# Column spreads as transposes of a broadcast column, logit columns inside the values' product, and a new static order in a four-layer graph network

## The chip, the cores and the metric

One core of one Trainium2 chip. The program is written engine by engine, with its semaphores and the order of all steps fixed by hand-kept tables. The metric is the device time of one execution in microseconds; lower is better.

## The reference

The input is 16 graphs of 512 nodes with 128 features, `x`, and an integer adjacency matrix `adj` (512 x 512 per graph). Four layers follow one another, each on a layer-normed, rectified copy of the residual stream:

```python
h = jnp.maximum(_layernorm(x, axis=-1), 0.0)
x = x + _L0_gnn_ref(h, adj, L0_gnn_W, L0_gnn_a)
h = jnp.maximum(_layernorm(x, axis=-1), 0.0)
x = x + _L1_gnn_ref(h, adj, L1_gnn_W, L1_gnn_b, L1_gnn_a)
h = jnp.maximum(_layernorm(x, axis=-1), 0.0)
x = x + _L2_gnn_ref(h, adj, L2_gnn_a0, L2_gnn_a1, L2_gnn_a2, L2_gnn_a3, L2_gnn_bias)
h = jnp.maximum(_layernorm(x, axis=-1), 0.0)
x = x + _L3_gnn_ref(h, adj, L3_gnn_weight, L3_gnn_w_ih, L3_gnn_w_hh, L3_gnn_b_ih, L3_gnn_b_hh)
```

The first layer is graph attention with one head, the second the same with four heads of 32 columns:

```python
Wh = jnp.einsum('bnf,of->bno', h, W)
s1 = Wh @ a1
s2 = Wh @ a2
e = jax.nn.leaky_relu(s1[:, :, None] + s2[:, None, :], negative_slope=ALPHA)
att = jax.nn.softmax(jnp.where(mask, -jnp.inf, e), axis=-1)
out = jnp.einsum('bij,bjo->bio', att, Wh)
```

`s1` is a number for each row of the logits (the source), `s2` one for each column (the target). The third layer takes a sigmoid of weighted inner products of the rows, chosen by the kind of edge, and the fourth runs three steps of a gated recurrent cell on the sums over neighbours.

## The kernel before, in words

A graph's 512 nodes lie as C = 4 chunks of 128 on the partitions. The work of a graph is cut into some 170 named steps in four stages: A (first layer), L (logits and softmax of the second layer), B (the rest of the second layer and the third), C (recurrent cell). All stages of different graphs overlap: while graph g is in C, graph g+1 is in L and B and graph g+2 in A. Each engine (TensorE, VectorE, ScalarE, GpSimd) runs the steps strictly in the order that `in_order` gives it: it sorts all steps of all graphs by `BEGIN[stage][graph] + WHEN[engine][step]`. These numbers are keys that set the order, not times. An engine whose next step isn't ready waits, with all that is queued behind it. SyncE loads `x` and the transposed adjacency, GpSimd the two other copies of the adjacency; ScalarE's queue issues the output's store (step `store`).

The steps that the text speaks of, with their lines:

- `rowsN` (N = 0 to 3) turns the normed rows: four transposes on TensorE (`turn_rows`, L936) after all four norm chunks (`normN_0` to `_3` on ScalarE, L394, after GpSimd's power and product, L363 and L365), then a copy to `hT` on ScalarE (L399).
- The logits need the target number spread over all 128 partitions: a row of 512 targets, the same in each partition. `dst0` (L961) and `dst1` to `dst4` (L1005) get it as a full product of the turned rows with `dst_rep`, the target's weight column repeated 128 times, into one PSUM bank; ScalarE copies it to `spread` (L411, L450).
- `src0` (L941 by `project`, four products of one column) gives the first layer's source numbers, which VectorE scales into `s1_lift` (L682); `values0` (L941, four products of 128 columns) gives the values, which ScalarE copies (L416). `values1` (L1009, L1013) gives the second layer's values and its four source columns, 132 columns a chunk, behind one tiny product for a count of edges; VectorE adds the bias (L739), scales the sources (L741) and reads the count (L746).
- `m`/`n` (VectorE, masked maximum, L642), `top`, `below`, `max` (tiny, L650 to L659), `u`/`v` (VectorE logits L663, then ScalarE's exponential L423, L460), `t`/`q` (TensorE, four transposes, L948, then ScalarE's copy to `pT`, L428, L468), `sum0`, `sum1` (L981, L1040).
- `x2` turns the second layer's result on TensorE (L1049), `scaled` and `x2` finish it on VectorE (L796, L802); `mean3` is the last VectorE step of the fourth layer norm (L638); `split` (ScalarE L508, VectorE L865) cuts the normed rows in two parts for `agg` (L1117, L1120), the sums over neighbours. `hidden_*` and `joint_*` (L1102, L1105) are the cell's products, `turn` (L1142) its state turned.
- `s`, `w` are the third layer's slope, hyperbolic tangent and products (L836, L492, L843, L1088); `z` (L1061) its inner products.

PSUM has eight banks. `a_bank` serves all of stage A one after the other, `l_bank0` and `l_bank1` all of stage L.

## Time and profile before

| | |
|---|---|
| three runs | 1064.18, 1065.93 (median), 1067.51 us |
| the profiled execution's own time | 1066.04 us |
| its span in the profile | 1063.9 us |
| granted TensorE clock, mean | 0.967 of 2.4 GHz |
| TensorE busy | 954.6 us (90%) |
| VectorE busy | 892.3 us (84%) |
| ScalarE busy | 864.0 us (81%) |
| GpSimd busy | 132.6 us (12%) |

Busy times are unions of an engine's instructions. Durations in a row hold an instruction's whole latency; instructions in a stream follow each other more closely than they last, so the rate of a stream is read from the chain of waits or the starts in the timeline. A TensorE product of fp32 shows as two matmul records, a transpose and an fp32r product as one.

### The profile page before, as it was taken

What the parts mean: (1) busy time and instruction counts of PE and PEld (TensorE: products, weight loads), DVE (VectorE), ACT (ScalarE), POOL (GpSimd) and SP (SyncE); (2) the same over time, 40 slices, a digit from 0 to 9 for tenths busy, and PEclk for the clock granted to TensorE, in tenths of its full rate; (3) what the DMA queues carried; (4) which work ended last, traced back from release to release, by engine and by line L of the source; (5) the groups of instructions that cost most, each with busy time, mean ns of one, the idle gap of its engine ahead of it and who ended that gap; (6) DMA issues with size and microseconds to landing.
All of it is one profiled execution on the core that took longest, in us unless ns stands there. A gap on an engine that the chain in (4) does not pass through costs nothing.

```text
span 1063.9 us, 16086 instructions
## 1 busy us (share of the span) xinstructions
PE 954.6 (90%) x5024; PEld 609.6 (57%) x5024; DVE 892.3 (84%) x2710; ACT 864.0 (81%) x1860; POOL 132.6 (12%) x170
## 2 busy tenths in 40 slices
PE   4588998999989899999989899998989999998866
PEld 3455565666566566656556566656656665655443
DVE  5296989899898979899897989989897989979543
ACT  3367888979888897988888897988889798887742
POOL 1102011010202011020201201020201101010000
PEclk8558999999999999999999999999999999999989
DMA  2401204021210403121220402121030302111000
GB/s 72 109 1 39 72 11 109 11 61 52 68 51 14 106 11 77 44 60 51 56 64 10 110 11 60 60 61 51 15 105 11 79 31 61 50 40 51 1 11 10
DMA packets 42477, 52.32 MB, mean 49 GB/s; under 512 B 1296, under 2 KB 25872, under 8 KB 42384
## 3 DMA queue, kind: packets, MB, share of 16 engines
q0 software_dynamic: 16896, 25.17, 10.7%
q1 hardware_dynamic: 17040, 21.83, 6.5%
q10 hardware_dynamic: 8448, 4.20, 1.3%
q8 instruction: 44, 0.72, 0.3%
q14 instruction: 49, 0.40, 0.1%
HBM read 55.39 MB, written 4.19 MB: 56 GB/s over the span
## 4 chain that ended last, share of the span: by engine, by line
PE 52%; DVE 28%; ACT 10%; issue 6%; POOL 3%; DMA 0%; DVEq 0%; SPq 0%; ACTq 0%; POOLq 0%
PE l_bank L948 7%; DVE probs L642 6%; PE a_bank L981 6%; PE x_bank L1040 4%; PE a_bank L948 3%; PE h_bank L1102 3%; ACT hn L394 3%; PE r_bank L1102 3%; PE r_bank L1105 3%; DVE sess L843 3%; DVE sess L836 3%; PE h_bank L1105 3%; PE n_bank L1105 3%; DVE probs L663 3%; POOL rstd L363 2%
## 5 line engine op out<-in xcount | busy, mean ns | idle before, releaser
L663 DVE SCALAR_TENSOR_TENSOR probs<-spread,s_lift,probs 128x512 f32<-128x512 f32 x320 | 237.4, 747 | 4.0 <-DVE rmax L642 0.5
L642 DVE CUSTOM_DVE_ANT_0 probs<-spread,mask 128x512 f32<-128x512 f32 x320 | 211.8, 684 | 2.4 <-ACT spread L450 2.3
L363 POOL TENSOR_TENSOR rstd<-var_eps,power 128x4 f32<-128x4 f32 x64 | 88.0, 1375 | 882.5 <-DVE var_eps L636 603.0
L460 ACT ACTIVATE probs<-probs,shift_p 128x512 f32<-128x512 f32 x256 | 185.7, 725 | 5.7 <-DVE shift_p L659 5.7
L468 ACT ACTIVATE pT<-l_bank 128x512 f32<-128x512 f32 x256 | 151.8, 600 | 46.5 <-PE l_bank L948 46.3
L948 PEld LDWEIGHTS l_bank<-ident,probs 128*128 128x128 f32 x1024 | 124.3, 144 | 73.8 <-issue 46.0
L948 PE MATMUL l_bank<-ident,probs 128*128 128x128 f32 x1024 | 150.5, 278 | 6.1 <-ACT probs L460 5.1
L394 ACT ACTIVATE hn<-x,shift,rstd 128x128 f32<-128x128 f32 x192 | 80.5, 492 | 26.1 <-POOL shift L365 26.0
L1005 PE MATMUL l_bank<-hT,dst_rep 128*128 128x512 f32 x128 | 73.6, 658 | 12.1 <-ACT pT L468 8.5
L870 DVE SCALAR_TENSOR_TENSOR hid_n<-r_t,hid_n 128x512 f32<-128x512 f32 x48 | 33.1, 689 | 57.8 <-ACT r_t L518 57.8
L981 PE MATMUL a_bank<-values,pT 128*128 128x128 f32 x512 | 65.7, 286 | 0.7 <-ACT pT L428 0.7
L1088 PE MATMUL y_bank<-hn,sess 128*128 128x128 f32 x512 | 61.6, 278 | 4.2 <-DVE sess L843 4.1
L1088 PEld LDWEIGHTS y_bank<-hn,sess 128*128 128x128 f32 x512 | 58.4, 192 | 11.9 <-DVE sess L843 11.9
L981 PEld LDWEIGHTS a_bank<-values,pT 128*128 128x128 f32 x512 | 63.0, 202 | 2.0 <-ACT pT L428 2.0
L1040 PE MATMUL x_bank<-pT,values 128*32 128x512 f32 x512 | 58.2, 595 | 0.7 <-ACT pT L468 0.7
L450 ACT ACTIVATE spread<-l_bank 128x512 f32<-128x512 f32 x64 | 38.4, 600 | 23.4 <-PE l_bank L1005 23.4
L948 PEld LDWEIGHTS a_bank<-ident,probs 128*128 128x128 f32 x256 | 29.9, 149 | 44.5 <-ACT pT L428 35.8
L948 PE MATMUL a_bank<-ident,probs 128*128 128x128 f32 x256 | 44.4, 300 | 9.7 <-ACT probs L423 5.6
L460 ACT ACTIVATION_READ_ACCUMULATOR probs<-probs,shift_p 128x1 f32 x256 | 51.8, 202 | 0.0
L1105 PE MATMUL r_bank<-aggT,gi_w 128*128 128x512 f32 x96 | 49.4, 596 | 0.0
L1105 PE MATMUL h_bank<-aggT,gi_w 128*128 128x512 f32 x96 | 49.1, 593 | 0.0
L1105 PE MATMUL n_bank<-aggT,gi_w 128*128 128x512 f32 x96 | 49.1, 593 | 0.0
(175 smaller groups left out, 1956.5 us busy)
## 6 DMA issues: line engine op xcount, KB each, us to landing
adjt_i<-in_adj_t SPq DMA_DIRECT2D x16, 1024.0 KB, 5.2
edges<-in_adj POOLq DMA_DIRECT2D x16, 1024.0 KB, 5.9
adj_h<-in_adj POOLq DMA_DIRECT2D x16, 512.0 KB, 7.7
xin<-in_x SPq DMA_DIRECT2D x16, 256.0 KB, 2.9
out<-out_sb ACTq DMA_DIRECT2D x16, 256.0 KB, 3.8
weights_sb<-in_weights SPq DMA_DIRECT2D x1, 840.0 KB, 4.7
```

The lines of the kernel that those rows point to most:

```text
L363: g.tensor_tensor(rstd[n][:], var_eps[n][:], power[:], op=ALU.pow).then_inc(pool_step[n], 1)
L394: s.activation(hn[n][:, c, :], rows[:, c, :], ACT.Relu, bias=shift[n][:, c:c + 1], scale=rstd[n][:, c:c + 1]).then_inc(hn_ready[n], 1)
L460: s.activation(row, row, ACT.Exp, bias=shift_p[:, head, c:c + 1], accum_out=den[:, head, c:c + 1]).then_inc(probs_ready, 1)
L468: s.activation(pT[:, head - 1, :, c * P:(c + 1) * P], l_banks[unit % 2][:, :].rearrange("p (j i) -> p j i", j=C), ACT.Copy).then_inc(pT_co ...
L642: return v.tensor_tensor_reduce(out=row, in0=spread_row, in1=mask, scale=1.0 / LIFT, scalar=-3e38, op0=ALU.subtract, op1=ALU.max, accum_ou ...
L663: v.scalar_tensor_tensor(row, spread_row, source, row, ALU.min, ALU.subtract, reverse1=True).then_inc(ready, 1)
L948: last = t.transpose(dst[:, j * P:(j + 1) * P], row[:, j * P:(j + 1) * P], ident[:])
L981: last = t.matmul(a_bank[:, c * P:(c + 1) * P], pT0[:, j, c * P:(c + 1) * P], values0[:, j, :], start=(j == 0), stop=(j == C - 1))
L1005: t.matmul(l_banks[head % 2][:, :], dst_rep[:, head, :], hT[1][:, :], start=True, stop=True).then_inc(dst_ready, 1)
L1040: last = t.matmul(x_bank[h * HD:(h + 1) * HD, :], values1[:, j, h * HD:(h + 1) * HD], pT[:, h, j, :], start=(j == 0), stop=(j == C - 1), s ...
L1088: last = t.matmul(y_bank[:, c * P:(c + 1) * P], sess[:, j, c * P:(c + 1) * P], hn[2][:, j, :], start=False, stop=(j == C - 1), skip_group_ ...
L1105: t.matmul(bank[:, :], gi_w[:, layer, gate * D:(gate + 1) * D], aggT[:, :], start=start, stop=True).then_inc(gi_ready, 1)
```

## The change

- Both layers' spreads are no products any more. The target numbers now come as a column of the values' product (so they lie on the partitions), and a spread is four transposes of that column read 128 times (`spread_column`).
- `values0_w` holds the value weights and two more columns (source, target, both scaled), 130 in all; `values1_w` eight more, 136 in all. The first layer's product doesn't fit in one bank, so its last chunk comes as a step of its own, `last0`, with its own ScalarE copy. The steps `src0` on TensorE and VectorE are gone, with `dst_rep` and `s1_lift`; the logits read the source from the values tile.
- `values1` on VectorE is two additions of 272 columns, without the two scalings.
- So `dst0` now follows `values0` and `last0`, and `dst1`, `dst2` follow VectorE's `values1`.
- `turn_rows` waits for each norm chunk in turn instead of for the fourth.
- The tables `BEGIN` and `WHEN` are new, and with them the order on each engine.

```diff
-A_STEPS = (["stats0", "aggr0", "mean0"] + [f"norm0_{c}" for c in range(4)] + ["rows0", "mask0", "dst0", "src0", "values0"] + [f"m{c}" for c in range(4)]
+A_STEPS = (["stats0", "aggr0", "mean0"] + [f"norm0_{c}" for c in range(4)] + ["rows0", "mask0", "values0", "last0", "dst0"] + [f"m{c}" for c in range(4)]
...
-    (1964, 49567, 56552, 63343, 70222, 76976, 83703, 90370, 97051, 103773, 110574, 117357, 124170, 130936,
+    (-52840, -43380, -37049, -30901, -24797, -18611, -12429, -6317, -207, 6011, 12192, 18291, 24388, 30591,
...
-                    s.activation(values0[:, :, :].rearrange("p c d -> p (c d)"), a_bank[:, :],
+                    s.activation(values0[:, 0:C - 1, :].rearrange("p c k -> p (c k)"), a_bank[:, 0:(C - 1) * COLS0],
                                  ACT.Copy).then_inc(val0_copied, 1)
+                elif step == "last0":
+                    act.wait_ge(last0_ready, p.count(1, 1))
+                    s.activation(values0[:, C - 1, :], a_bank[:, 0:COLS0], ACT.Copy).then_inc(last0_copied, 1)
...
-                elif step == "src0":
-                    dve.wait_ge(src0_ready, p.count(1, 1))
-                    v.tensor_scalar(s1_lift[:, 0, :], a_bank[:, 0:C], -LIFT, None, ALU.mult).then_inc(s10_copied, 1)
...
                     for half in range(2):
-                        both = l_banks[half][:, 0:2 * (D + H1)].rearrange("p (c k) -> p c k", c=2)
-                        pair = slice(2 * half, 2 * half + 2)
-                        v.tensor_tensor(values1[:, pair, :], both[:, :, 0:D],
-                                        b1_rows[:, :].unsqueeze(1).to_broadcast([P, 2, D]), ALU.add)
-                        last = v.scalar_tensor_tensor(s1_lift[:, 1:HEADS, pair],
-                                                      both[:, :, D:D + H1].rearrange("p c h -> p h c"), -LIFT,
-                                                      head_const[:, :].unsqueeze(2).to_broadcast([P, H1, 2]),
-                                                      ALU.mult, ALU.subtract)
-                    last.then_inc(val1_copied, 1)
+                        both = l_banks[half][:, 0:2 * COLS1].rearrange("p (c k) -> p c k", c=2)
+                        v.tensor_tensor(values1[:, 2 * half:2 * half + 2, :], both,
+                                        b1_rows[:, :].unsqueeze(1).to_broadcast([P, 2, COLS1]),
+                                        ALU.add).then_inc(val1_copied, 1)
...
             def turn_rows(p, n, dst):
-                pe.wait_ge(hn_ready[n], p.count(C, C))
                 for c in range(C):
+                    pe.wait_ge(hn_ready[n], p.count(C, c + 1))
                     last = t.transpose(dst[:, c * P:(c + 1) * P], hn[n][:, c, :], ident[:])
                 last.then_inc(hT_ready[n], 1)
...
+            def spread_column(dst, columns, k, ready):
+                for c in range(C):
+                    last = t.transpose(dst[:, c * P:(c + 1) * P], columns[:, c, k:k + 1].to_broadcast([P, P]), ident[:])
+                last.then_inc(ready, 1)
...
+                elif step == "values0":
...
+                    for c in range(C - 1):
+                        last = t.matmul(a_bank[:, c * COLS0:(c + 1) * COLS0], hT[0][:, c * P:(c + 1) * P],
+                                        values0_w[:, :], start=True, stop=True)
+                    last.then_inc(val0_ready, 1)
+                elif step == "last0":
+                    pe.wait_ge(val0_copied, p.count(1, 1))
+                    t.matmul(a_bank[:, 0:COLS0], hT[0][:, (C - 1) * P:], values0_w[:, :], start=True,
+                             stop=True).then_inc(last0_ready, 1)
                 elif step == "dst0":
-                    if not p.before().exists():
-
-                        pe.wait_ge(w_step, 9)
-                    pe.wait_ge(hT_copied[0], p.count(1, 1))
-                    t.matmul(a_bank[:, :], dst_rep[:, 0, :], hT[0][:, :], start=True, stop=True).then_inc(dst0_ready, 1)
-                elif step == "src0":
-                    pe.wait_ge(dst0_copied, p.count(1, 1))
-                    project(0, a_bank, 1, src_w[:, 0:1], src0_ready)
-                elif step == "values0":
-                    pe.wait_ge(s10_copied, p.count(1, 1))
-                    project(0, a_bank, D, w0t_sb, val0_ready)
+                    pe.wait_ge(last0_copied, p.count(1, 1))
+                    spread_column(a_bank, values0, D + 1, dst0_ready)
...
                 elif step[:3] == "dst":
                     head = int(step[3])
-                    if head == 1:
-                        pe.wait_ge(hT_copied[1], p.count(1, 1))
-                        if prev.exists():
-                            pe.wait_ge(pT_copied, prev.count(UNITS, UNITS))
-                    elif head == 2:
+                    if head < 3:
+                        pe.wait_ge(val1_copied, p.count(2, 2))
                         pe.wait_ge(others_ready, p.count(1, 1))
-                        pe.wait_ge(val1_copied, p.count(1, 1))
                     else:
                         pe.wait_ge(pT_copied, p.count(UNITS, (0, 0, 0, 2, 5)[head]))
-                    t.matmul(l_banks[head % 2][:, :], dst_rep[:, head, :], hT[1][:, :], start=True,
-                             stop=True).then_inc(dst_ready, 1)
+                    spread_column(l_banks[head % 2], values1, TARGET1 + head - 1, dst_ready)
                 elif step == "values1":
+                    pe.wait_ge(hT_copied[1], p.count(1, 1))
                     pe.wait_ge(count_ready, p.count(1, 1))
+                    if prev.exists():
+                        pe.wait_ge(pT_copied, prev.count(UNITS, UNITS))
                     t.matmul(l_bank0[:, COUNT_AT:COUNT_AT + 1], ones[:], count[:, 0:1], start=True, stop=True)
-                    pe.wait_ge(dst_copied, p.count(H1, 1))
```

Three places of the order matter to the text. First TensorE around the fourth layer norm of a graph in mid-program. Before:

```order
L1088 MATMUL y_bank<-hn,sess 128x128 x16
L948 MATMUL l_bank<-ident,probs 128x128 x8
L941 MATMUL a_bank<-weights_sb,hT 128x128 x4
L948 MATMUL l_bank<-ident,probs 128x128 x8
L1005 MATMUL l_bank<-hT,dst_rep 128x512
L936 MATMUL x_bank<-ident,hn 128x128 x4
L1117 MATMUL n_bank<-edges,state_hi 128x512 x4
```

and now, at the same place of the program:

```order
L1069 MATMUL y_bank<-hn,sess 128x128 x16
L928 MATMUL l_bank<-ident,probs 128x128 x16
L923 MATMUL l_bank<-ident,values 128x128 x4
L918 MATMUL x_bank<-ident,hn 128x128 x4
L1098 MATMUL n_bank<-edges,state_hi 128x512 x4
```

The first layer's values (L941) have moved from here to before the third layer's inner products, and the spread of the fourth head (`dst4`) is four transposes, so between `w` and `agg` there are only transposes left.

Second TensorE at the end of the second layer's sums, ahead of the turn of the result (`avT`). Before:

```order
L1040 MATMUL x_bank<-pT,values 32x512 x16
L936 MATMUL l_bank<-ident,hn 128x128 x4
L1142 MATMUL h_bank<-ident,state 128x128 x4
L1049 MATMUL y_bank<-ident,avT 128x128 x4
L1005 MATMUL l_bank<-hT,dst_rep 128x512
L1102 MATMUL r_bank<-state,weights_sb 128x512
L1009 MATMUL l_bank<-count,ones 128x1
L1013 MATMUL l_bank<-values_w,hT 128x132 x4
```

and now:

```order
L1021 MATMUL x_bank<-pT,values 32x512 x8
L918 MATMUL l_bank<-ident,hn 128x128 x4
L1021 MATMUL x_bank<-pT,values 32x512 x8
L991 MATMUL l_bank<-count,ones 128x1
L994 MATMUL l_bank<-values_w,hT 128x136 x4
L1030 MATMUL y_bank<-ident,avT 128x128 x4
L1123 MATMUL h_bank<-ident,state 128x128 x4
L923 MATMUL l_bank<-ident,values 128x128 x4
```

The count and the values of the next graph now stand ahead of the turn of this graph's result; on VectorE the step `values1` likewise stands just ahead of `scaled`, where it used to come after `stats2`. The turned state (L1142, now L1123) stands behind the result's turn in about two thirds of the graphs.

Third ScalarE in two stretches of the same graph: after the fourth norm, and at the copy of the second layer's sums. Before:

```order
L468 ACTIVATE pT<-l_bank 128x4x128
L394 ACTIVATE hn<-x,shift,rstd 128x128 x4
L508 ACTIVATE state_hi<-hn 128x512
...
L394 ACTIVATE hn<-x,shift,rstd 128x128 x4
L522 ACTIVATE z_t<-n_bank,gate_b 128x512
L526 ACTIVATE n_t<-hid_n,gate_b 128x512
L441 ACTIVATE counted,count<-adj_h,minus_half 128x2048
L476 ACTIVATE avT<-x_bank 128x512
L399 ACTIVATE hT<-l_bank 128x512
```

and now:

```order
L378 ACTIVATE hn<-x,shift,rstd 128x128 x4
L538 DMA out<-out_sb 128x4x128
L495 ACTIVATE state_hi<-hn 128x512
...
L428 ACTIVATE counted,count<-adj_h,minus_half 128x2048
L509 ACTIVATE z_t<-n_bank,gate_b 128x512
L383 ACTIVATE hT<-l_bank 128x512
L513 ACTIVATE n_t<-hid_n,gate_b 128x512
L378 ACTIVATE hn<-xin,shift,rstd 128x128 x2
L463 ACTIVATE avT<-x_bank 128x512
```

The store's issue has moved from before the fourth norm to between it and the split, and the copy of the next graph's turned rows and two chunks of the first norm of the graph after that now stand ahead of the copy of `avT`.

## Rows read from the trace of the kernel before

**Rows 1.** The page's second part, granted TensorE clock in tenths over 40 slices; one instruction's record.

```profile
PEclk8558999999999999999999999999999999999989
...
L508 ACT ACTIVATE state_hi<-hn x16: 630/631/632, 123.7 to 1025.6; 128x512 fp32r<-128x512 f32 x16
```

**Rows 2.** Stretches: length, busy PE, PEld, DVE, ACT, POOL, PEclk, DMA share, GB/s.

```profile
426.00:486.80 60.80, 57.33 (x314) 36.82 (x314) 54.91 (x168) 53.41 (x117) 8.96 (x10) 1.00 0.21 54
...
489.20:519.30 30.10, 30.09 (x177) 19.08 (x178) 25.11 (x76) 29.30 (x65) 3.99 (x4) 1.00 0.03 9
519.40:545.20 25.80, 23.87 (x120) 15.69 (x119) 25.50 (x79) 19.87 (x44) 3.21 (x4) 1.00 0.31 66
```

**Rows 3.** Chain of waits, one graph in mid-program: start us, us, what.

```profile
484.80 1.41 POOL rstd L363
...
489.19 1.16 PE n_bank L1117 x4
...
492.00 0.86 PE r_bank L1102 x2
...
493.72 0.44 PE l_bank L948 x4
...
519.46 0.70 DVE x L796
...
522.74 0.33 DVE values L739
...
545.02 0.17 DVE var_eps L638
```

**Rows 4.** Groups of instructions, shapes apart: name, shape, count, busy us, mean ns, idle before.

```profile
L1005 PE MATMUL l_bank<-hT,dst_rep 128*128 128x512 f32 x128 | 73.6, 658 | 12.1 <-ACT pT L468 8.5 <-DVE other_kinds L746 2.3 <-ACT hT L399 1.3
...
L741 DVE SCALAR_TENSOR_TENSOR s_lift<-l_bank,head_const 128x8 f32<-128x8 f32 x32 | 5.0, 156 | 0.0
```

**Rows 5.** Chain of waits in the first 72 us, at the 1.2 GHz level from 20.5.

```profile
11.37 2.05 PE a_bank L961 x2
...
24.04 1.10 PE a_bank L948 x4
...
46.76 2.09 PE l_bank L1005 x2
...
60.39 1.50 PE a_bank L941 x8
```

**Rows 6.** Timeline of TensorE in the wait for the fourth norm: start us, us, what, idle before.

```profile
481.75 1.04 PE L948 MATMUL l_bank<-ident,probs 128*128 128x128 f32 x8
484.15 1.16 PE L941 MATMUL a_bank<-weights_sb,hT 128*128 128x128 f32 x8 [1.36 <-DVE s_lift L682]
...
486.48 1.12 PE L1005 MATMUL l_bank<-hT,dst_rep 128*128 128x512 f32 x2 [0.30 <-ACT pT L468]
488.44 0.65 PE L936 MATMUL x_bank<-ident,hn 128*128 128x128 f32 x4 [0.84 <-ACT hn L394]
```

**Rows 7.** Stretches around changes of the granted clock, columns as in rows 2.

```profile
71.70:75.10 3.40, 1.83 (x12) 1.35 (x12) 3.37 (x13) 3.29 (x8) 0.00 (x0) 0.95 0.00 0
88.80:91.80 3.00, 1.76 (x12) 1.26 (x12) 2.90 (x17) 2.97 (x7) 0.55 (x1) 1.00 0.25 73
...
481.70:489.10 7.40, 4.90 (x32) 3.36 (x31) 7.37 (x31) 6.01 (x14) 1.76 (x2) 1.00 0.58 178
1024.00:1030.80 6.80, 5.18 (x14) 4.02 (x15) 0.69 (x1) 3.39 (x7) 0.00 (x0) 0.52 0.00 0
```

**Rows 8.** Timeline of TensorE after its longest idle time.

```profile
1025.62 1.11 PE L936 MATMUL x_bank<-ident,hn 128*128 128x128 f32 x4 [5.56 <-ACT hn L394]
```

**Rows 9.** Timeline of ScalarE, same graph.

```profile
485.35 0.38 ACTq L551 DMA_DIRECT2D out<-out_sb  x1
...
486.74 1.65 ACT L394 ACTIVATE hn<-x,shift,rstd 128x128 f32<-128x128 f32 x4 [0.31 <-POOL shift L365]
...
517.95 0.60 ACT L476 ACTIVATE avT<-x_bank 128x512 f32<-128x512 f32 x1
```

More of the change, by code:

```diff
@@ L643, in masked_max, with sources @@
                                               op0=ALU.subtract, op1=ALU.max, accum_out=top)
+            def sources(head):
+                return values1[:, :, SOURCE1 + head - 1] if head else values0[:, :, D]
             def shift_part(p, head, part):
@@ L768, in step_l @@
                     if unit == 0:
[L769 removed]
+                        dve.wait_ge(val1_copied, p.count(2, 2))
                     if c == 0:
                         dve.wait_ge(max_ready[1], p.count(H1, head))
[L772 removed]
+                    source = values1[:, c, SOURCE1 + head - 1:SOURCE1 + head]
+                    logits(probs[:, head % 2, c, :], spread[:, head % 2, :], source, logits_ready)
             def kinds_of(p, k):
```

88 lines of the change are left out of this document (40 added, 48 removed), and 119 rows, old and new, of the table WHEN.

## The prediction

> **What bounds the kernel now.** I read three views in this order: stretches of a graph in mid-program, the chain of waits, and the records of the instructions that the change touches.
>
> The stretches show three engines that are all nearly full: in 60.8 us TensorE is busy for 57.3, VectorE for 54.9, ScalarE for 53.4 [rows 2]. Such shares don't say who sets the pace. The chain does. In every graph in mid-program it has the same shape [rows 3]: the last VectorE step of the fourth norm ends, GpSimd takes its power at 484.8, ScalarE norms and splits, and TensorE starts `agg` at 489.2. From there TensorE is the chain without a gap until it has turned the second layer's result, and VectorE starts `scaled` at 519.5. From there VectorE is the chain until it ends the next graph's fourth norm at 545.2. That is 4.4 + 30.3 + 25.7 = 60.4 us, and the split of the norm comes round 16 times between 123.7 and 1025.6, some 60.1 us apart [rows 1]. So each half has a rate-setter: TensorE in the first (30.09 busy of 30.1), VectorE in the second (25.50 of 25.8), while the other engine of each half has slack: VectorE 25.1 of 30.1, TensorE 23.9 of 25.8 [rows 2]. ScalarE is nearly as full as TensorE in the first half (29.30). Work that is removed pays only in the half where its engine sets the pace.
>
> No spread and no projection stands in the TensorE part of the chain in mid-program. They all lie in the half that VectorE sets. This is what decides the forecast. Before 124 us it is otherwise: there the graphs don't overlap yet, and spreads and projections are on the chain, half of the time at the lower clock [rows 5].
>
> **The change part by part.**
>
> *Five spreads a graph.* A product of 512 fp32 columns holds TensorE for 0.86 us, by the same shape in the chain, four transposes for 0.44 [rows 3]; the 0.66 us of a spread's record [rows 4] is the latency of one of its two passes. TensorE gives up 5 x 0.42 = 2.1 us a graph. No row shows a transpose of a column read 128 times. I take the price of the plain transpose, whose instruction has the same shape; the lower end is the same, the upper end the product's 0.86 (no gain). The four `src0` products take 1.5 us at the lower clock [rows 5], 0.8 to 0.9 at the full one. In mid-program these 3 us a graph fall in TensorE's slack: worth nothing by themselves.
>
> *The start.* Up to 72 us the chain holds six spreads of about 2.05 us at the lower clock, where four transposes take 1.10 to 1.13, and `src0` twice (0.8 and 1.5) [rows 5]: 6 x 0.9 + 2.3 = 7.7 us. Against it, graph 0 now has `values0`, two copies and `last0` ahead of its spread, some 3 us; the three gate products, which stood between spread and `src0`, come off the chain (3.6 us). Later parts of the start are held by exponentials and copies, so I take 5 us off; bounds 8 off and 2 on (2 on if the clock, with less work on TensorE, rises after 92 us instead of at 85).
>
> *The order, TensorE's half.* The next graph's count and values (nine short products, 1.0 us) now stand ahead of the result's turn, a turn of the state (0.44) leaves in two thirds of the graphs: +0.6 to +1.05. VectorE's `values1` stands ahead of `scaled` and needs these products; it ends 0.35 us after the turned result would be ready. ScalarE gets a copy (0.6), two norm chunks (2 x 0.41) and the store's issue (0.38) ahead of `avT` [rows 9], 1.8 us in a stretch in which it had about 1 us to spare. The store delays `agg`'s first half by 0.4, of which VectorE's own split, due at about the same time as before, hides half. Together `scaled` starts 1.0 us later in the loop; bounds 0.3 and 1.8.
>
> *The order, VectorE's half.* `values1` leaves it: two additions (0.33 each [rows 3]) and three short instructions (at most 0.16 each [rows 4]), 0.9 us; `src0`, 0.12 us, is gone. That is 1.0 us less; with TensorE ahead of need, some of the half's waits go too (25.7 against 25.5 busy, so 0.2). Bounds 0.7 and 1.6.
>
> *Turning by chunk.* Each `rowsN` can end 0.3 us sooner, since three of four transposes run before the last chunk is there. After the fourth norm `agg` waits for the split, not for these turns; nothing. Queued behind the partial wait is only TensorE work that would wait anyway.
>
> Loop: +1.0 - 1.2 = -0.2 us a graph, 14 graphs: -3 us (bounds -18 and +15).
>
> *The clock.* Between `w` and `agg` TensorE waits for the fourth norm. Until now that wait was well filled: 32 records, 4.9 us of 7.4, and the clock stayed at 2.4 GHz [rows 7], with eight product records at 484.15 and a spread at 486.48 [rows 6]. Both the values and half the spread's time are gone from it: 24 transposes are left, 2.6 us in 7.4, most of them early, so that from a good microsecond after VectorE's last step to `agg` there are only the four turns. The two nearest rows disagree by a little: at 71.7 to 75.1 twelve transposes in 3.4 us (eight together, four after a gap) went before a fall to 1.2 GHz; at 88.8 to 91.8 twelve in 3.0, evenly, went without [rows 7]. The new stretch is thinner than both. After a fall TensorE isn't back at once: at the end it restarted at 1025.62 [rows 8] and ran at 1.2 GHz until 1030.8, 5.2 us, losing 2.6. The shortest low stretch is 3.4 us, a loss of 1.7 or, where half of it falls in the wait, 0.85. This loss lands at the head of TensorE's own half, where nothing hides it. I take 1.4 us in 8 of 14 graphs: +11 (bounds 0 and 14 x 2.6 = +36).
>
> The Trainium skill (TensorE: Matmul & The Clock Gate, Part 4) says that transposes don't count as TensorE activity for the clock. The stretch from 88.8 to 91.8, transposes alone at the full clock, speaks against it. By the rule every graph would lose the clock and the time would be that of the second rival.
>
> **Sum.** 1066.0 (the profiled execution: span 1063.9 and 2.1 around it; 0.1 above the median) - 5 - 3 + 11 = **1069 us**, no change within 0.3%, which is about what a measurement of this kernel can tell. Own range of this case 1060 to 1077.
>
> **The rivals.**
>
> *The clock holds.* For it: mid-program never shows a fall before, in 14 waits, and a transpose seems to count. Against: the stretch is thinner than any that kept the clock. Then 1066 - 5 - 3 = 1058.
>
> *The clock falls in every graph, slower.* Place: the wait for the fourth norm; price: 1.6 us each on TensorE's half, 14 times, 22 us: 1066 - 5 - 3 + 22 = 1080. It decides once the clock falls in more than about 8 of the 14 waits. For it: the wait is the same in each graph. Against: 88.8 to 91.8, and the two nearest stretches that came out differently. The Trainium skill's rule of Part 4 would have it so.
>
> *The clock holds and the loop tightens.* If ScalarE absorbs what stands ahead of `avT`, and VectorE's half loses all its waits, the loop gives 1.1 us: 1066 - 5 - 15 = 1046. For it: TensorE, 3 us lighter, serves the other two earlier. Against: both halves are one engine's ordered work, which the new order changes little.
>
> *The broadcast column is slow to read.* At 0.86 us a spread nothing is won at the start but `src0`, and the wait stays fuller: 1066 - 2 + 2 = 1066.
>
> **How the numbers follow.** Chances: forecast 0.38, clock holds 0.28, clock falls everywhere 0.17, loop tightens 0.12, slow column 0.05. Faster by over 0.3% (below 1062.8): 0.26 of the second, all of the fourth, 0.06 of the forecast, 0.01: 0.45. Slower (above 1069.2): 0.17 and 0.20 of the forecast and 0.01: 0.38. Within: 0.17. The range takes 1046 to 1082: beyond it lie half of the tight loop (0.06) and a third or so of the falls everywhere (0.06). The forecast's own range stands above, since both signs hold much.
>
> **What would show it.** In the profile after: four-transpose spreads at 0.44 us in the chain or timeline, no L941-like group of one column, VectorE's values at 272 columns; the chain again TensorE from `agg` to the turned result, then VectorE from `scaled`, halves near 31.3 and 24.5 us. The granted clock decides: fives or eights and sevens scattered through the second part of the page, and `agg` records of double length, mean the forecast or the rule; nines throughout mean 1058 or less. The forecast is wrong if the clock is at 2.4 GHz throughout and the time still above 1062, or if the chain leaves the two halves.

## The result, and the profile after

The changed kernel takes **1083.94 us** (median of 4 runs, 1083.19 to 1084.75); the kernel before, run beside it, 1065.06 us (4 runs, 1063.36 to 1067.51). The ratio is 1.0176, 95% interval 1.0152 to 1.0199: slower by 1.5 to 2.0%. The profiled execution took 1083.28 us, with a span of 1081.2. All marks, stretches and chains below come from the one profiled execution of a kernel; the ratios come from all its runs.

The page of the changed kernel, first and second part (columns as on the page before; PEclk is [rows 1]'s line):

```profile
span 1081.2 us, 16130 instructions
PE 945.9 (87%) x5056; PEld 613.1 (57%) x5056; DVE 896.0 (83%) x2658; ACT 869.0 (80%) x1876; POOL 134.2 (12%) x170
...
PEclk9658999999999999998999999899999999999989
```

TensorE is busy 8.7 us less than before, VectorE 3.7 and ScalarE 5.0 us more, and the span is 17.3 us longer, so more work on an engine isn't enough to explain it. The clock line shows two eights in mid-program where [rows 1] has nines only. The record of the fourth norm's split, to be set beside that of [rows 1]:

```profile
L495 ACT ACTIVATE state_hi<-hn x16: 629/630/632, 122.7 to 1042.9; 128x512 fp32r<-128x512 f32 x16
```

Its first start is 1.0 us earlier, its last 17.3 later: 920.2 us for 15 periods against 901.9. What follows the last split takes 38.3 us in both. So **the start gave 1.0 us and the 15 periods behind it cost 18.3**.

Stretches of one graph, from one fourth norm's last VectorE step to the next, and its two halves, as [rows 2] has them for a graph before:

```profile
427.30:489.20 61.90, 56.31 (x315) 36.19 (x315) 55.35 (x165) 53.63 (x118) 8.59 (x10) 1.00 0.19 52
431.70:463.50 31.80, 31.63 (x186) 20.11 (x186) 26.36 (x80) 30.71 (x68) 3.26 (x4) 1.00 0.03 10
463.50:489.20 25.70, 21.64 (x114) 14.24 (x113) 24.59 (x74) 18.64 (x39) 3.61 (x4) 1.00 0.28 66
```

The clock is at its full level here. TensorE's half has grown by 1.7 us, and TensorE is busy in all of it with nine records more; in VectorE's half TensorE lost 2.2 us of work, which changed little, as VectorE sets that half. The end of TensorE's half in the chain of waits of the same graph (start us, us, what):

```profile
457.00 1.85 PE x_bank L1021 x16
458.86 0.59 PE l_bank L918 x4
459.45 1.85 PE x_bank L1021 x16
461.30 0.31 PE l_bank L991 x2
461.62 1.03 PE l_bank L994 x8
462.65 0.49 PE y_bank L1030 x4
```

and VectorE's timeline behind it:

```profile
462.69 0.79 DVE L724 TENSOR_TENSOR values<-l_bank,b_rows 128x272 f32<-128x272 f32 x2
463.39 0.15 DVE L727 TENSOR_SCALAR other_kinds<-l_bank 128x1 int32<-128x1 f32 x1
463.46 0.68 DVE L778 TENSOR_TENSOR x<-y_bank,rden 128x512 f32<-128x512 f32 x1
464.17 0.69 DVE L784 TENSOR_TENSOR x<-x 128x512 f32<-128x512 f32 x1
...
466.16 0.68 DVE L628 CUSTOM_DVE_ANT_0 probs<-spread,mask 128x512 f32<-128x512 f32 x1
```

Between the second layer's sums (L1021) stand the next graph's turned rows (0.59), and between the sums and the result's turn (L1030) its count and values (0.31 + 1.03). VectorE copies the values (L724) before it may scale (L778), and has its first masked maximum (L628) 2.7 us after `scaled`.

The same marks in every graph from the second to the fourteenth, in us after the norm's last VectorE step (means). Graphs in which the clock was low somewhere between `agg` and the next norm are left out; a fall that was over before `agg` leaves its graph in:

| kernel | sums end | `scaled` starts | next norm | VectorE's half | graphs |
|---|---|---|---|---|---|
| before | 33.05 | 34.85 | 60.75 | 25.90 | 13 |
| changed | 34.12 | 36.61 | 61.72 | 25.11 | 11 |

TensorE's half +1.76, VectorE's -0.79, together **+0.97 us a graph**. In the changed kernel the clock fell in the wait in six of the 13 graphs. In four of them it was back at its full level before `agg`; in the other two it was low until 9.0 and 9.2 us after the norm's last VectorE step, well into the products behind the wait. One of these two, TensorE's timeline in the wait for the fourth norm, beside [rows 6]:

```profile
486.39 1.04 PE L928 MATMUL l_bank<-ident,probs 128*128 128x128 f32 x8
489.48 0.66 PE L928 MATMUL l_bank<-ident,probs 128*128 128x128 f32 x4 [2.06 <-ACT probs L447]
490.67 0.66 PE L928 MATMUL l_bank<-ident,probs 128*128 128x128 f32 x4 [0.53 <-ACT probs L447]
491.16 0.95 PE L923 MATMUL l_bank<-ident,values 128*128 128x128 f32 x4
491.90 1.46 PE L918 MATMUL x_bank<-ident,hn 128*128 128x128 f32 x4
493.64 2.05 PE L1098 MATMUL n_bank<-edges,state_hi 128*128 128x512 f32 x4 [0.28 <-ACT state_hi L495]
```

No product is left in the wait, the clock is at 1.2 GHz within the records from 491.16 on, and `agg`'s first half takes 2.05 us where [rows 3] has 1.16. The stretch around it, columns as in [rows 7] (the third figure from the end is the granted clock, 0.60 of the full one in the mean):

```profile
490.00:497.00 7.00, 6.19 (x22) 4.40 (x21) 7.00 (x20) 6.24 (x15) 1.01 (x2) 0.60 0.42 149
```

The last of the 15 periods, which the table leaves out, takes 53.50 us where it took 51.75. It has a low stretch too, from 1003.4 to 1006.8 us, and that one lies on TensorE's part of the chain; the first line below is a product that takes 0.86 elsewhere:

```profile
1003.77 1.71 PE r_bank L1083 x2
1005.48 0.85 PE l_bank L928 x4
1006.34 1.19 PE h_bank L1098 x4
```

At the full level these three take 0.86, 0.44 and 0.93, so some 1.5 us of that period's 1.75 are the clock's.

### The profile page after: what moved, and what is told of

Read it like the earlier page. It is cut to its first block, busy times and chain, and to the rows that moved or that the text cites. A ratio compares the mean times of both kernels' runs of the same rounds, so it can differ in the third digit from the quotient of the medians.

```text
span 1081.2 us, 16130 instructions
## 1 busy us (share of the span) xinstructions
PE 945.9 (87%) x5056; PEld 613.1 (57%) x5056; DVE 896.0 (83%) x2658; ACT 869.0 (80%) x1876; POOL 134.2 (12%) x170
## 4 chain that ended last, share of the span: by engine, by line
PE 42%; DVE 29%; ACT 18%; issue 7%; POOL 3%; DMA 0%; DVEq 0%; SPq 0%; ACTq 0%; POOLq 0%
DVE probs L628 8%; PE l_bank L928 5%; ACT probs L447 5%; PE x_bank L1021 5%; DVE probs L652 3%; PE r_bank L1083 3%; PE r_bank L1086 3%; ACT hn L378 3%; PE n_bank L1086 3%; DVE sess L818 3%; PE a_bank L928 2%; DVE stats L609 2%; PE n_bank L1083 2%; DVE sess L825 2%; ACT pT L455 2%
## 5 line engine op out<-in xcount | busy, mean ns | idle before, releaser
L652 DVE SCALAR_TENSOR_TENSOR probs<-spread,values,probs 128x512 f32<-128x512 f32 x320 | 237.4, 747 | 2.1
L628 DVE CUSTOM_DVE_ANT_0 probs<-spread,mask 128x512 f32<-128x512 f32 x320 | 212.4, 683 | 9.7 <-ACT spread L395 6.1
L928 PE MATMUL l_bank<-ident,probs 128*128 128x128 f32 x1024 | 161.4, 288 | 47.4 <-ACT probs L447 43.8
L347 POOL TENSOR_TENSOR rstd<-var_eps,power 128x4 f32<-128x4 f32 x64 | 83.6, 1306 | 898.7 <-DVE var_eps L622 638.8
L1021 PE MATMUL x_bank<-pT,values 128*32 128x512 f32 x512 | 60.9, 598 | 0.7 <-ACT pT L455 0.7
L918 PE MATMUL x_bank<-ident,hn 128*128 128x128 f32 x128 | 40.8, 348 | 16.3 <-ACT hn L378 12.2
L923 PE MATMUL l_bank<-ident,values 128*128 128x128 f32 x256 | 43.0, 298 | 9.6 <-ACT pT L455 6.8
```

The source lines that it names most:

```text
L347: g.tensor_tensor(rstd[n][:], var_eps[n][:], power[:], op=ALU.pow).then_inc(pool_step[n], 1)
L628: return v.tensor_tensor_reduce(out=row, in0=spread_row, in1=mask, scale=1.0 / LIFT, scalar=-3e38, op0=ALU.subtract, op1=ALU.max, accum_ou ...
L652: v.scalar_tensor_tensor(row, spread_row, source, row, ALU.min, ALU.subtract, reverse1=True).then_inc(ready, 1)
L928: last = t.transpose(dst[:, j * P:(j + 1) * P], row[:, j * P:(j + 1) * P], ident[:])
L1021: last = t.matmul(x_bank[h * HD:(h + 1) * HD, :], values1[:, j, h * HD:(h + 1) * HD], pT[:, h, j, :], start=(j == 0), stop=(j == C - 1), s ...
```

## The experiments

Two theories stood against each other, and a third beside them. **Order**: the new order put the next graph's rows, count and values into TensorE's half. **Operations**: a spread that reads VectorE's copy of the values comes later than one that reads the turned rows, whatever the order. **Clock**: the wait, emptied of products, lets the clock fall. Ratios are to runs of the kernel before on the same chip; below, a diff's `+` is the experiment.

### The new operations in the old order, two variants

The steps take the old steps' places by key: the values where a spread stood, the spread where the values stood, `last0` behind the third layer's second inner product (`z1`) of the graph two before, and VectorE's third-norm moments behind the copy of the values. The variants differ in the place of layer 1's first spread on TensorE (ScalarE's copy of it moves along); the tables are given in words, `...` stands for the other engines:

```diff
-BEGIN, WHEN of the changed kernel
+BEGIN, WHEN of the kernel before, values0 <-> dst0, values1 <-> dst1 on TensorE
+MOVED = {'tensor': [('last0', -2, 'z1')], ...}                              # spread ahead of the aggregate
+MOVED = {'tensor': [('last0', -2, 'z1'), ('dst1', -2, 'g2_agg')], ...}      # spread behind it
```

> The changed kernel's operations (spreads as turned columns, logit columns with the values, rows turned by chunk) in the order of the kernel before: each new step takes the place of the step that it replaces, the values stand in the place of the old spreads, the spreads in the place of the old values; layer 1's first spread is put behind the old graph's third aggregate. Theory order (the new order puts the next graph's rows, count and values into TensorE's half, ahead of the turned result): the loop goes back to some 60.8 us, less what the lighter TensorE gives, so 1055 to 1065. Theory operations (the spread now hangs on VectorE's copy of the values, whatever the order, so the first masked maximum starts later): a loop still 1 us longer, 1075 or more. In this variant the aggregate, some 2 us of TensorE, stands ahead of that spread, so up to 1.9 us more per graph could come on top by the second theory: up to 1100.

> As the run before, but with layer 1's first spread ahead of the third aggregate, in the very place of the old values. Theory order: 1055 to 1065. Theory operations: 1075 or more. If both theories hold in part, this one is the faster of the two variants by up to 1.9 us a graph, since VectorE waits for this spread with its first masked maximum, and the aggregate has nobody waiting so soon.

Spread ahead: 1092.19 us, ratio 1.0249 (1.0225 to 1.0272). Spread behind the aggregate: 1127.39 us, 1.0579 (1.0554 to 1.0603). The theory of the order alone has fallen: TensorE's half was back to the old one (33.00 and 34.75 us in the table further down), and still a graph without a fall took 61.54 us, 0.8 more than before. That this run is slower than the changed kernel as a whole says nothing about the order, since in the same seven graphs the new order takes 61.64 us (read from the filled version below, which has no fall there); the difference lies in the clock and at the two ends of the program. VectorE's timeline of the variant with the spread ahead, a graph in which the clock held:

```profile
468.39 0.69 DVE L790 TENSOR_TENSOR x<-y_bank,rden 128x512 f32<-128x512 f32 x1 [1.82 <-PE y_bank L1042]
...
471.10 0.77 DVE L736 TENSOR_TENSOR values<-l_bank,b_rows 128x272 f32<-128x272 f32 x2
471.79 0.14 DVE L739 TENSOR_SCALAR other_kinds<-l_bank 128x1 int32<-128x1 f32 x1
...
472.34 0.16 DVE L634 TENSOR_SCALAR var_eps<-moments 128x4 f32<-128x4 f32 x1
473.37 0.69 DVE L640 CUSTOM_DVE_ANT_0 probs<-spread,mask 128x512 f32<-128x512 f32 x1 [0.88 <-ACT spread L449]
```

and TensorE's, where the spread stands:

```profile
469.28 1.02 PE L1095 MATMUL r_bank<-state,weights_sb 128*128 128x512 f32 x2
472.08 0.62 PE L935 MATMUL l_bank<-ident,values 128*128 128x128 f32 x4 [1.79 <-DVE other_kinds L739]
```

For comparison, the kernel before at that place:

```profile
522.25 0.42 DVE L739 TENSOR_TENSOR values<-l_bank,b_rows 128x256 f32<-128x256 f32 x1
...
523.13 0.37 DVE L629 BATCH_NORM_AGGREGATE moments<-stats 128x2 f32<-128x6 f32 x4
523.41 0.66 DVE L642 CUSTOM_DVE_ANT_0 probs<-spread,mask 128x512 f32<-128x512 f32 x1
```

There the first masked maximum starts 3.95 us after `scaled` without a wait; here 4.98 after, behind a wait of 0.88. TensorE stood idle 1.79 us for VectorE's copy, turned it, ScalarE copied the spread, and VectorE waited for that. The graph costs 61.54 us (7 graphs), 0.79 more than before. In five of 13 graphs the clock was low as well in TensorE's half (1.1 to 2.3 us each), in a sixth in VectorE's. With the aggregate ahead of the spread it is 63.10 in the two graphs without a fall, and there are 20 low stretches, 102 us in all, in mid-program: my limit of 1100 left these out, so it was a miss.

### One spread as a product again

Old order, all new operations but layer 1's first spread. It is a product of the turned rows again and stands ahead of the values, in its old place, and VectorE's third-norm moments are back in theirs:

```diff
                     head = int(step[3])
+                    if head == 1:
+                        pe.wait_ge(hT_copied[1], p.count(1, 1))
...
+                        t.matmul(l_bank1[:, :], dst_rep1[:], hT[1][:, :], start=True, stop=True).then_inc(dst_ready, 1)
+                        return
```

> The changed kernel's operations in the old order, but layer 1's first spread is again the product of the replicated column with the turned rows, ahead of the values, as in the kernel before; the other four spreads are turned columns. Theory latency (what the old order lost against the kernel before in VectorE's half, 0.9 to 1.0 us a graph, is the wait of the first masked maximum for a spread that now needs VectorE's own copy of the values): that wait goes, the time from one fourth norm to the next without a fall of the clock is 60.6 to 60.9 us in place of 61.6, and 13 us of the 27 go: 1076 to 1080. The falls of the clock in the wait for the fourth norm stay, as in the run of the old order (8 to 10 us in five graphs). Theory that the other new operations are what costs (272-column values, chunkwise turns, layer 0): still 61.6 us, 1090.

1078.7 us, ratio 1.014 (1.0121 to 1.016), some 12 us less by the two ratios, as expected. In the five graphs without a fall a period takes 60.43 us. The theory of the latency of this one spread holds: undoing it, with its place, takes 1.1 us off each graph. What remained over the kernel before was the clock: nine low stretches in mid-program, seven of which reach into TensorE's half. These counts are of the fastest of the four runs (1072.55 us, mean clock 0.956); the other three were granted 0.941 to 0.945.

### The clock

Three products into the hole before VectorE's masked maxima, in the changed kernel:

```diff
                     turn(l_banks[unit % 2], probs[:, head % 2, c, :], turned)
+                    if unit == 3 and p.graph >= 2:
+                        for _ in range(3):
+                            t.matmul(r_bank[:, 0:3 * D], ident[:], w_iht_sb[:], start=True, stop=True)
```

> The changed kernel with three products of 384 fp32 columns, from constants and into a bank that is free then, put behind the turn that TensorE does just before it waits for VectorE's masked maximum in the wait for the fourth norm (a hole of 2.2 us, which they fill; nobody reads what they write). Theory clock: the clock no longer falls in mid-program and the three graphs that lost 1.0 to 2.0 us to it in the profile don't: 1079, 5 us less than the changed kernel. Theory order alone: no change, 1084. If the products delay anything, it is at most 0.2 us a graph, 3 us.

1079.68 us, ratio 1.0131 (1.0107 to 1.0155), 4.3 us less. The intervals of the two ratios touch, but the traces settle it: no wait of these 13 graphs has a fall any more, and every graph has the same marks to 0.1 us as in the changed kernel except the two in which the clock had been low behind `agg`, which took 61.65 and 61.95 in place of 63.29 and 63.73. TensorE's timeline of the first of them:

```profile
486.93 2.10 PE L1012 MATMUL r_bank<-weights_sb,ident 128*128 128x384 f32 x6
489.15 0.66 PE L928 MATMUL l_bank<-ident,probs 128*128 128x128 f32 x4
...
493.31 1.16 PE L1101 MATMUL n_bank<-edges,state_hi 128*128 128x512 f32 x4 [0.42 <-ACT state_hi L495]
```

The same in the version with one product spread, with two products for three:

```diff
+                    if unit == 3 and p.graph >= 2:
+                        for _ in range(2):
```

> As the run before, and with two products of 384 fp32 columns into a free bank in the wait for the fourth norm, which nobody reads. Theory clock: no fall in mid-program, and 8 to 10 us less than the run before; with both theories right this is the kernel before less what the change gives at the start (1 to 4 us): 1060 to 1066. If the clock theory is wrong, no difference to the run before.

A miss: 1080.76 us, ratio 1.0138 (1.0099 to 1.0177), no better. The clock now fell in 12 of 13 graphs; the low stretches began mostly 3.9 to 5.1 us after the norm's last VectorE step, where those of the changed kernel had begun 0.3 to 2.4 us after it, so I took the late part of the wait for the thin one. A second pair went right ahead of the turned rows of the fourth norm:

```diff
                     spread_column(l_banks[head % 2], values1, TARGET1 + head - 1, dst_ready)
+                    fill(2 if head == 4 and p.graph >= 2 else 0)
```

> The kernel of the run with one product spread (old order, five graphs in six with a fall of the clock or close to it), now with two unread products of 384 fp32 columns in each of two holes of the wait for the fourth norm: behind the turn before VectorE's masked maxima, as in the run that failed to hold the clock, and behind head 4's spread, right before the turns of the fourth norm's rows. In that failed run the low stretches began 3.2 to 5.1 us after VectorE's last step of the norm, so it was the late part of the wait that was thin. Theory clock: no fall in mid-program, 60.3 to 60.6 us from norm to norm, and with the 2 us that this version gains at the start 1055 to 1062: faster than both kernels. Theory that the falls have another cause than the thin wait: 1075 to 1081 again.

1064.12 us over 12 runs, ratio **0.9997 (0.9985 to 1.0009)**: 15 us less than with no filler, with no fall in any wait of mid-program, and level with the kernel before, not faster, where I had expected 1055 to 1062. TensorE in that wait:

```profile
422.55 0.66 PE L946 MATMUL l_bank<-ident,probs 128*128 128x128 f32 x4 [0.32 <-ACT probs L460]
423.52 0.65 PE L937 MATMUL l_bank<-ident,values 128*128 128x128 f32 x4 [0.32 <-ACT pT L468]
424.01 1.46 PE L942 MATMUL r_bank<-weights_sb,ident 128*128 128x384 f32 x4
425.30 0.73 PE L932 MATMUL x_bank<-ident,hn 128*128 128x128 f32 x4
426.46 1.17 PE L1122 MATMUL n_bank<-edges,state_hi 128*128 128x512 f32 x4 [0.42 <-ACT state_hi L508]
```

The wait's length (3.70 to the split, 4.48 to `agg`) is the same with and without the products: they cost nothing. Two low stretches are left, both in VectorE's half; beside the same graphs of the next run, where they have none, they cost 1.2 and 1.4 us. This run has both more products in the wait and products in its late part, so it doesn't tell number from place. A fifth product between the two pairs:

```diff
+                    fill({3: 2, 5: 1}.get(unit, 0) if p.graph >= 2 else 0)
```

> As the run with both holes filled, and one product more between them, behind the turn before head 4's spread. If two holes are enough, this gives the same time or 0 to 3 us more (it delays that spread by up to 0.2 us, which VectorE needs later): 1055 to 1064. If the clock still falls with two, it is less or none here, and this one is the faster.

1065.03 us, 1.0003 (0.9989 to 1.0018): the same, 1 us above what I had expected, again with two falls in VectorE's half.

The other way round, the kernel before with its wait emptied. From the third graph on it leaves out three of the four products of layer 0's values, so its output is another:

```diff
-                    project(0, a_bank, D, w0t_sb, val0_ready)
+                    if p.graph < 2:
+                        project(0, a_bank, D, w0t_sb, val0_ready)
+                    else:
+                        t.matmul(a_bank[:, 0:D], hT[0][:, 0:P], w0t_sb, start=True, stop=True).then_inc(val0_ready, 1)
```

> The kernel before, untouched but for three of the four products of layer 0's values, which are left out from the third graph on (1.3 us less of TensorE inside the wait for the fourth norm, on nobody's chain; layer 0's output is another). Theory clock: TensorE does less and the program gets slower, with low stretches in the wait in 3 to 13 of the 14 graphs and 4 to 20 us on top: 1069 to 1085. Theory that the changed kernel's falls come of something else: no fall, 1062 to 1065.

1065.91 us, 1.0015 (1.0001 to 1.003). Less TensorE work, and the clock falls in four waits of mid-program where it never fell before: taking products out of the wait does let it fall. But each fall delayed `agg`'s second half by at most 0.2 us and cost the graph nothing measurable (60.44 us in one with a fall, 60.44 in the same graph of the run with rows turned by chunk): 1.6 us in all where I had expected at least 4. What a fall costs hangs on how far it reaches into the products behind the wait: here it ended within 0.9 us of `agg`'s start, in the two dear graphs of the changed kernel 4.6 and 4.8 us behind it.

### Undoing pieces of the new order

First the count and the values behind the result's turn on TensorE, and their copy behind x2 on VectorE; then also the turned rows behind the sums, and their copy on ScalarE behind `avT`:

```diff
+MOVED = {'tensor': [('values1', -1, 'x2'), ('dst1', -2, 'g2_hidden_r')],
+         'vector': [('values1', -1, 'x2'), ('stats2', 1, 'values1'), ('aggr2', 0, 'stats2'), ('mean2', 0, 'aggr2'), ('dst1', -1, 'mean2')]}
+# second: 'tensor' also ('rows1', -1, 'sum1_3'), 'scalar': [('rows1', -1, 'x2')]
```

> The changed kernel with one piece of its order undone: on TensorE the next graph's count and values go behind the turn of the second layer's result, on VectorE the copy of the values goes behind x2, with the third norm's sums ahead of the first masked maximum. Theory of two halves: TensorE's half gets 1.0 to 1.5 us shorter (the scaled result starts at 35.2 in place of 36.2 to 37.1 after the fourth norm), VectorE's half takes back the copy (0.8) and the wait for the spread that was seen in the old order (0.9): some 0 to +0.5 us a graph in all, 1083 to 1092. If only what stands ahead of the scaled result counts, 1.2 us a graph less: 1066 to 1070.

> As the run before, and the turn of layer 1's rows goes behind the last sum as well, its copy behind that of the sums on ScalarE: all four things that the new order put into TensorE's half are out of it but the exponentials' waits. TensorE's half another 0.6 to 0.7 us shorter (sums end at 33.4 in place of 34.05); but the values then wait for the rows' copy, 0.6 us later. By the theory of two halves 1080 to 1092, as the old order with the new operations (1092); by the theory that only TensorE's half counts 1057 to 1062.

1108.86 us, ratio 1.0422 (1.0405 to 1.044), and 1107.17 us, 1.0385 (1.0358 to 1.0411): both worse than either expectation. The marks of the graphs without a fall account for 13 us of what the first of the two loses on the changed kernel; the expectations had left out the clock, whose falls between `agg` and the next norm cost some 11 and 12 us in these two runs where the changed kernel loses 3.4. All marks together (graphs chosen and means taken as above):

| kernel | sums end | `scaled` starts | next norm | VectorE's half | graphs |
|---|---|---|---|---|---|
| before | 33.05 | 34.85 | 60.75 | 25.90 | 13 |
| changed | 34.12 | 36.61 | 61.72 | 25.11 | 11 |
| changed, filled | 34.11 | 36.61 | 61.73 | 25.12 | 13 |
| values behind the turn | 34.04 | 36.26 | 62.72 | 26.46 | 5 |
| rows and values back | 33.48 | 35.92 | 62.76 | 26.84 | 6 |
| old order | 33.00 | 34.75 | 61.54 | 26.79 | 7 |
| old order, one product | 33.00 | 34.78 | 60.43 | 25.65 | 5 |
| the same, both holes filled | 33.04 | 34.88 | 60.60 | 25.72 | 11 |

What TensorE's half gets back (0.35, then 0.69 us), VectorE's half loses two to four times over (1.35, 1.73). With these operations it looks like one trade: either the values stand in TensorE's half and the spread is there in time, or they don't and VectorE waits for it. In both orders a graph costs 0.8 to 1.0 us more than before; moving single pieces of the new order costs another 1.0. Of the kernels tried only those with the old kind of first spread, which needs no copy of VectorE, escape it, and they have the old order: the new order with that one product was not run, so that the new order's 0.97 us would go with it is argued, not shown.

The means of the last rows are over different graphs. Over the eleven graphs of the last row the kernel before takes 60.84 us, so that version is 0.24 us a graph faster than before, and its two falls in VectorE's half (1.2 and 1.4 us) take most of that back.

### Rows turned by chunk, alone

```diff
-                pe.wait_ge(hn_ready[n], p.count(C, C))
                 for c in range(C):
+                    pe.wait_ge(hn_ready[n], p.count(C, c + 1))
```

> The kernel before with one part of the change alone: rows turned chunk by chunk as each chunk's norm ends, its order untouched. I expect no change, 1062 to 1068, and so does every theory that blames the order or the clock. A theory that the waits by chunk cost TensorE's queue something (three more waits in each of 64 turns) would give 3 us or more on top, 1069.

1067.37 us over 12 runs against 1065.61, ratio 1.0007 (0.9989 to 1.0026): no change, as expected.

### The start filled

Unread products of 256 columns where TensorE waits in the first 70 us, on top of the version with both holes filled:

```diff
+                        for _ in range(5 if p.graph == 0 else 0):
+                            fill_start()
```

These five stand behind graph 0's layer-0 sums; two more stand behind its turned rows of layer 1, one behind its values, and one behind each turned row of probabilities until the first gate product.

> The version with both holes filled (level with the kernel before), with unread products of 256 fp32 columns added where TensorE waits in the first 70 us or so: five behind graph 0's layer-0 sums, two behind its turned rows of layer 1, one behind its values, one behind each turn of a probability row until the first gate product. In that version 58 us before the first split of the fourth norm ran at 1.2 GHz. Theory: the low clock at the start is kept up by TensorE's waits, and the chain there is partly TensorE's, so with the waits filled the clock rises earlier and the first split comes 3 to 10 us sooner: 1054 to 1061, faster than both kernels. Rival: the products, 0.87 us each at the low clock, delay the turns that ScalarE and VectorE wait for, and the clock stays low: 1064 to 1075.

A miss: 1066.36 us, 1.0016 (0.9994 to 1.0038), with runs from 1062.3 to 1071.6. The time at the low clock before the first split fell from 58.0 to 37.5 us, and the first split came at 124.0 in place of 122.9: TensorE had more of the full clock and nothing was won. Whether the products' own time ate the gain or VectorE and ScalarE hold the start wasn't tried apart.

## Why the prediction was wrong

The time came out 2 us above the range, and 15 above the forecast. By its own steps:

*The two halves.* Right for the first: TensorE from `agg` to the turned result, with no spread or projection of the kernel before in it. The second is less clean than I wrote. In two graphs of the kernel before the chain stays on TensorE after `scaled` and holds spreads and values; in one of them it runs over two spreads of layer 1 (397.87 and 403.45 us) and one of layer 0 (407.97), 0.9 us each. Right was the price of a spread, 0.44 us for four turned columns: this row of the changed kernel's chain stands in the middle of other TensorE work.

```profile
465.61 0.44 PE l_bank L923 x4
```

Its worth in mid-program was small, as forecast, if not nothing: the version with four cheap spreads, no `src0` and the waits filled needs 60.60 us a graph where the kernel before needs 60.84 in the same eleven graphs.

*The start, -5.* Measured -1.0. I listed what `values0` and its copies put ahead of layer 0's spread, but priced layer 1's by its duration alone. Chain of the changed kernel:

```profile
43.65 0.49 ACT hT L383
44.18 0.59 PE l_bank L991 x2
44.77 2.04 PE l_bank L994 x8
...
47.83 1.10 PE l_bank L923 x4
48.95 0.61 ACT spread L437
```

and of the kernel before, of whose spread [rows 5] has the record at 46.76:

```profile
46.22 0.49 ACT hT L399
...
48.87 0.61 ACT spread L450
```

At the turned rows' copy the changed kernel is 2.6 us ahead; it then needs count, values, VectorE's copy and the turn, 4.8 us where one product took 2.1, and at the copied spread it is level. First splits of kernels with nearly the same start scatter (120.0, 122.5 and 123.7 us for the kernel before and its two near copies), so the term's size is known to 3 or 4 us only, and it isn't sure that the start gained at all.

*TensorE's half, +1.0 (bounds 0.3 and 1.8).* Measured +1.76, within the bounds but at the upper one. I had counted count and values with 1.0, less a turn of the state in some graphs, and VectorE's copy with 0.35; in the chain above they are 1.34 and 0.32. I missed the turned rows between the sums: the run that moved them and their copy brought the sums' end forward by 0.56, half of the 1.07 by which they end late; the other half stays open. The store's issue, which I had given 0.2 us, cost nothing: `agg` starts 4.43 us after the norm's last VectorE step, before 4.48.

*VectorE's half, -1.2 (bounds 0.7 and 1.6).* Measured -0.79: the right sign, and two thirds of the size.

*The loop, -0.2 a graph, -3.* Measured +0.97 a graph, 12.6 us in 13 graphs; with the rest of the two periods at the ends some 13.4. **This is the step that failed**: a term forecast as a gain of 3 us was a loss of 13. By sizes, TensorE's half was 0.76 us a graph too small and VectorE's gain 0.41 too large. Behind the sizes stands a step left out of the reasoning. I took the two halves as independent edits, one plus, one minus, and priced the spreads as slack. The new operations bring a dependency, values to VectorE's copy to spread, which I never followed to VectorE's first masked maximum. The runs show that in the old order it costs 0.8 us a graph, and that undoing it for one spread of five takes all of that away. That the new order's 1.0 us is the same dependency, paid in TensorE's half, fits the marks and the two runs with pieces moved back, but no run undoes it there.

*The clock, +11.* Right in kind, too large. I had put 1.4 us in each of 8 waits; the clock fell in 6 of 13, and only two of them lost anything, 1.6 and 1.8 us, since in the four others the low stretch was over before `agg`. The fall of the last period, in the middle of TensorE's half, where I had none, cost about 1.5. Together 4.9 us. With no fall in the waits the changed kernel still takes 1079.7, against my sentence that a holding clock means 1058.

*The sum in full.* 1066.0 - 1.0 + 13.4 + 4.9 = 1083.3, the profiled execution's 1083.28. It closes because the loop's ends are taken as what is left; what was measured apart are the start, the 13 graphs (12.6) and the two dear falls (3.4).

*The rivals.* The one whose time came nearest (1080) had the wrong reason. Its clock cost 22 us; the runs give the clock 5 and the loop 13. By the Trainium skill (TensorE: Matmul & The Clock Gate, Part 4) transposes don't count as TensorE activity for the clock in the way other products do. In each of the 13 graphs of the changed kernel TensorE has nothing but the same 24 transposes in the 7.1 us before `agg`, yet in seven of them the clock didn't fall at all, and in four more it was back when `agg` began. The traces don't bear out that every such wait loses the clock. That work in the wait matters, the filled and the emptied versions show; what picks the graphs in which it falls, among waits with the same work, no run shows. Open as well is why two products early in the wait held nothing in one order where three held the clock in the other.

*No gain anywhere.* The best version with the new operations is level with the kernel before. The 3 us of TensorE that it saves a graph lie nearly all in slack, as the prediction had it.

## What to carry to other kernels

When an operation is replaced by a cheaper one, write down what it reads and who makes that, and price the new path from the common source to the consumer, not the two durations: here four transposes at 0.44 us replaced a product of 0.86, and the path to the consumer got 1.0 us longer in the loop (old order) and 2.7 us longer at the start. A cost of the order in one half and a gain in the other may be the two sides of one dependency; undo the dependency, not the order, to see it. And before removing work from a wait of TensorE, read the granted clock around it: work that hides in the wait may be what keeps the clock, and unread products in its place cost nothing in the waits tried here.

## What was not expected of the hardware

- A column read 128 times costs TensorE what a plain transpose does: 0.44 us for four in the chain, and a record of it lasts 292 to 298 ns in the mean, in four of the five groups of plain ones 288 to 298.
- Unread products can hold the clock: two early in the wait left 12 falls in 13 graphs, two more in its late part left none in any wait. No run had four early ones or the two late ones alone, so whether the place or the number did it isn't shown.
- The same wait can lose the clock in one graph and keep it in the next: 24 transposes in 7.1 us each time, falls in 6 of 13.
- With 20 us more of the first 124 at TensorE's full clock, the first split came no earlier (124.0 us, before 122.9).
